# A four-layer graph network on one core: Adj turned a quarter at a time, rows of layer 1 one block nearer to use, bias added in layer 0

## The reference, cut to what matters

```python
# layer 0
gt = adj.T;  deg = gt.sum(1);  d = deg ** -0.5
x = x + (d[:, None] * gt * d[None, :]) @ (h @ W0) + bias
# layer 1
head = (adj > 0) / max(sqrt(row sum of (adj > 0)), 1e-12)
inc = adj + head
x = x + (inc @ h) / inc.sum(-1, keepdims=True)
# layer 2, four heads, the mean of them is added
ht = h @ W;  e = leaky_relu(src[i] + dst[j], 0.01) + adj
x = x + mean over heads of softmax(e) @ ht
# layer 3
x = x + relu(adj @ (binary(h) @ sign(W3).T))
```

## Time and profile before

| | us |
|---|---|
| median of three runs | 764.24 (764.19, 764.24, 768.5) |
| the profiled execution, whole | 766.52 |
| its span | 764.7 |
| mean granted TensorE clock in it | 0.964 |
| TensorE busy | 697.5 |
| VectorE busy | 632.3 |
| ScalarE busy | 480.7 |
| GpSimd busy | 112.5 |

### The profile page before, as it was taken

How to read it: one execution, slowest core, us unless ns; L and a number is a source line. 1 busy time by engine, 2 the same in 40 slices (tenths; PEclk the granted TensorE clock), 3 DMA queues, 4 the chain that set the end, 5 groups by cost and what they waited for, 6 DMA issues and landing times.

```text
span 764.7 us, 16125 instructions
## 1 busy us (share of the span) xinstructions
PE 697.5 (91%) x6480; PEld 587.6 (77%) x6480; DVE 632.3 (83%) x1165; ACT 480.7 (63%) x830; POOL 112.5 (15%) x146
## 2 busy tenths in 40 slices
PE   3988999959999999999990399999999999999998
PEld 3665888848889874488880388887888888888887
DVE  6997687788998737899980499997999999998683
ACT  4996333667887227975540487657686786776751
POOL 4432121311123210011212100211000000000000
PEclk9997999988999999999995699999999999999999
DMA  9886999497879768689999994999411612026591
GB/s 329 304 291 222 426 423 292 173 221 206 183 243 247 163 169 219 173 171 268 254 245 280 313 206 111 206 255 282 167 30 29 193 56 56 4 81 194 203 395 64
DMA packets 146457, 159.54 MB, mean 209 GB/s; under 512 B 90896, under 2 KB 103888, under 8 KB 141904
## 3 DMA queue, kind: packets, MB, share of 16 engines
q1 hardware_dynamic: 127328, 117.10, 51.6%
q0 software_dynamic: 19056, 41.42, 23.6%
HBM read 76.15 MB, written 52.46 MB: 168 GB/s over the span
## 4 chain that ended last, share of the span: by engine, by line
PE 52%; DMA 16%; DVE 15%; ACT 7%; issue 4%; SPq 3%; POOL 2%; ACTq 0%; POOLq 0%; DVEq 0%
DMA adj_t<-arena 8%; PE ps L829 8%; PE ps L831 8%; PE ps L830 8%; PE ps L769 5%; DMA arena<-adj_t 4%; PE ps L871 3%; PE ps L872 3%; DVE arena L1488 3%; DVE arena L1495 3%; DMA arena<-adj_parts 3%; SPq L383 2%; DVE arena L1260 2%; PE ps L717 2%; PE ps L719 2%
## 5 line engine op out<-in xcount | busy, mean ns | idle before, releaser
L829 PE MATMUL ps<-arena 128*128 128x257 f16 x1024 | 280.6, 274 | 32.5 <-DVE arena L1495 32.2
L831 PE MATMUL ps<-arena 128*128 128x257 f16 x1024 | 280.1, 274 | 0.0
L830 PE MATMUL ps<-arena 128*128 128x257 f16 x1024 | 280.0, 273 | 0.0
L1174 ACT ACTIVATE arena<-arena 128x512 f16<-128x512 f32 x252 | 158.2, 628 | 93.5 <-PE ps L831 62.4
L1495 DVE TENSOR_TENSOR arena<-arena 128x512 f16<-128x512 f32 x256 | 175.9, 688 | 40.4 <-ACT arena L1174 40.1
L1488 DVE SCALAR_TENSOR_TENSOR arena<-arena,w_j 128x512 f32<-128x512 f32 x256 | 190.3, 744 | 0.0
L829 PEld LDWEIGHTS ps<-arena 128*128 128x128 f16 x1024 | 100.2, 98 | 47.0 <-ACT arena L1174 33.4
L830 PEld LDWEIGHTS ps<-arena 128*128 128x128 f16 x1024 | 100.5, 98 | 12.7
L831 PEld LDWEIGHTS ps<-arena 128*128 128x128 f16 x1024 | 100.1, 98 | 13.2
L717 PE MATMUL ps<-arena 128*128 128x257 f16 x256 | 71.1, 278 | 3.6 <-DVE arena L1312 3.6
L719 PE MATMUL ps<-arena 128*128 128x257 f16 x256 | 70.5, 275 | 0.0
(11 more groups left out here) (155 smaller groups left out, 1115.6 us busy)
## 6 DMA issues: line engine op xcount, KB each, us to landing
adj_t<-arena POOLq DMA_DIRECT2D x32, 1024.0 KB, 8.3
arena<-in_adj_dram SPq DMA_DIRECT2D x32, 512.0 KB, 6.0
arena<-in_adj_dram SPq DMA_DIRECT2D x16, 1024.0 KB, 5.2
adj_parts<-arena SPq DMA_DIRECT2D x16, 1024.0 KB, 25.8
arena<-adj_t SPq DMA_DIRECT2D x64, 256.0 KB, 6.1
arena<-adj_t SPq DMA_DIRECT2D x16, 1024.0 KB, 7.1
x<-arena POOLq DMA_DIRECT2D x15, 512.0 KB, 6.2
arena<-u_rows SPq DMA_DIRECT2D x4, 1024.0 KB, 14.2
```

Of the source, the lines that this page charges most:

```text
L829: mm(ps[:, bank, 0:DE], hi, ht_hi[:, head, j, 0:DE], start=s, stop=False)
L830: mm(ps[:, bank, 0:DE], hi, ht_lo[:, head, j, 0:DE], start=False, stop=False)
L831: ins = mm(ps[:, bank, 0:DE], lo, ht_hi[:, head, j, 0:DE], start=False, stop=e)
L1174: nc.scalar.activation(p_hi[:, j % 4, :], prob[:, j % 4, :], copy).then_inc(p_hi_done, 1)
```

## The change

Four things are edited.

1. SP turns groups 4 to 7, loads e of quarter 1, turns 8 to 11, loads quarter 2, turns 12 to 15, loads quarter 3, and issues the two early loads of layer 3 last. WIDEN_AFTER spreads the widenings over heads 0 to 9 instead of 0 to 5; its waits on the pieces of quarter 3 ahead of the early loads go, as `load_e(3)` has them.
2. In layer 1 sign, count, fill, transposes and parts of a row come one iteration later than before (t + 5, t + 5, t + 4, t + 3, t + 3), and row 5 isn't counted in layer 0 any more. The five buffers stay.
3. TensorE multiplies groups 0 to 2 of rows 0 and 1, then group 3 of row 0, then group 3 of row 1.
4. The bias tile lies over `hrelu` instead of in g_hi's area. It is loaded after Adj, ahead of the writes of `nat`, once h @ W0 has read `hrelu`. GpSimd adds it after the powers of the degrees and before the loop with `inverse_root1`; VectorE waits for each tile's add in layer 0, and ScalarE no longer waits for it.

```diff
-        b0_bc = view(G0 + 7 * KB, [D], F32)
         hrelu = view(160 * KB, [2, D], F32)
+        b0_bc = view(160 * KB, [D], F32)
...
-        COUNTS = (1, 2, 9, 10, 11, 14)
+        COUNTS = (1, 2, 9, 10, 11)
...
-        WIDEN_AFTER = {0: (6, 7), 1: (8, 9), 2: (10, 11), 4: (12, 13), 5: (14, 15)}
+        DMA_ROWS = ()
+        PE_ROWS = [t for t in range(AHEAD, NB) if t not in DMA_ROWS]
+        WIDEN_AFTER = {0: (6,), 1: (7,), 3: (8,), 4: (9, 10), 5: (11,), 7: (12,), 8: (13, 14), 9: (15,)}
...
-            sp.dma_start(b0_bc, b0_d.partition_broadcast(P)).then_inc(bias_in, 16)
...
             for t in range(2):
                 load_rows(t)
+            sp.wait_ge(h0_lo_done, NB)
+            sp.dma_start(b0_bc, b0_d.partition_broadcast(P)).then_inc(bias_in, 16)
...
-            for n in range(QB, 3 * QB):
-                turn_adj(n)
             for q in range(1, NQ):
-                if q == 2:
-                    for n in range(3 * QB, 4 * QB):
-                        turn_adj(n)
-                if q == NQ - 1:
-                    for g in range(TG):
-                        sp.wait_ge(wide[g], 16 * NQ)
-                    for i in range(2):
-                        sp.dma_start(adjt_early[i], adjt_dram[i]).then_inc(adjt_in[4 + i], 16)
+                for g in range(TG):
+                    turn_adj(QB * q + g)
                 load_e(q)
+            for i in range(2):
+                sp.dma_start(adjt_early[i], adjt_dram[i]).then_inc(adjt_in[4 + i], 16)
...
-            pool.wait_ge(bias_in, 16)
-            for t in range(NB):
-                pool.wait_ge(relu0, t + 1)
-                nc.gpsimd.tensor_tensor(x[:, t, :], x[:, t, :], b0_bc, ALU.add).then_inc(bias_added, 1)
             pool.wait_ge(deg_copied, 1)
             for lo, hi in DINV_PIECES:
                 nc.gpsimd.tensor_tensor(dinv_in[:, lo:hi], deg[:, lo:hi], neg_half[:, lo:hi], ALU.pow
                                         ).then_inc(dinv_done, 1)
+            pool.wait_ge(bias_in, 16)
+            for t in range(NB):
+                nc.gpsimd.tensor_tensor(x[:, t, :], x[:, t, :], b0_bc, ALU.add).then_inc(bias_added, 1)
...
-                if t + 6 < NB:
-                    inverse_count(t + 6)
+                if t + 5 < NB:
+                    inverse_count(t + 5)
...
-            for t in range(NB):
+            for groups in (range(NB // TG - 1), (NB // TG - 1,)):
+                for t in range(2):
+                    for g in groups:
+                        products1(t, g)
+            for t in range(2, NB):
                 for g in range(NB // TG):
-                    if AHEAD <= t + 4 < NB:
-                        transpose_group(t + 4, g)
+                    if t + 3 in PE_ROWS:
+                        transpose_group(t + 3, g)
                     products1(t, g)
...
-            act.wait_ge(bias_added, NB)
...
             for t in range(NB):
-                more = AHEAD <= t + 4 < NB
+                more = t + 3 in PE_ROWS
                 if more:
-                    part_high(t + 4, 0)
-                if t + 6 < NB:
-                    sign(t + 6)
+                    part_high(t + 3, 0)
+                if t + 5 < NB:
+                    sign(t + 5)
...
-            dve.wait_ge(bias_added, NB)
-
             def layer0(t):
                 b = t % 2
+                dve.wait_ge(bias_added, t + 1)
                 dve.wait_ge(y_ps, t + 1)
...
-                if t + 5 < NB:
-                    fill(t + 5)
+                if AHEAD <= t + 4 < NB:
+                    fill(t + 4)
```

More of the change, by code:

```diff
@@ L687, in transpose_group @@
             def transpose_group(t, g):
-                n = 4 * (t - AHEAD) + g
+                n = 4 * PE_ROWS.index(t) + g
                 if g == 0:
@@ L703, in products1 @@
                 bank = ACC[t % 3]
-                if t >= AHEAD:
-                    pe.wait_ge(part_lo_done, 4 * (t - AHEAD) + g + 1)
+                if t in PE_ROWS:
+                    pe.wait_ge(part_lo_done, 4 * PE_ROWS.index(t) + g + 1)
                 elif g == 0:
-                    pe.wait_ge(inc_in[t], 32)
+                    pe.wait_ge(inc_in[t % AHEAD], 32 * (t // AHEAD + 1) if t < AHEAD else 64)
                 if g == 0 and t >= 3:
@@ L774, in _ @@
             pe.wait_ge(w2_lo_done, 4)
-            pe.wait_ge(part_lo_done, 4 * (NB - AHEAD))
+            pe.wait_ge(part_lo_done, 4 * len(PE_ROWS))
             pe.wait_ge(l1_taken, NB - 1)
@@ L1024, in _ @@
             for t in range(NB):
-                more = AHEAD <= t + 4 < NB
+                more = t + 3 in PE_ROWS
                 if more:
-                    part_high(t + 4, 0)
-                if t + 6 < NB:
-                    sign(t + 6)
+                    part_high(t + 3, 0)
+                if t + 5 < NB:
+                    sign(t + 5)
                 if more:
-                    part_high(t + 4, 1)
+                    part_high(t + 3, 1)
                 if t >= 2:
@@ L1034, in _ @@
                 if more:
-                    part_high(t + 4, 2)
+                    part_high(t + 3, 2)
                 if t >= 1:
@@ L1038, in _ @@
                 if more:
-                    part_high(t + 4, 3)
-                if t + 6 < NB:
-                    count(t + 6)
+                    part_high(t + 3, 3)
+                if t + 5 < NB:
+                    count(t + 5)
                 if t == 0:
@@ L1358, in fill @@
                     dve.wait_ge(nat_sent[1], 32)
-                if t >= AHEAD + 2:
-                    dve.wait_ge(t_ps, 4 * (t - AHEAD - 2) + 4)
+                if t - 2 in PE_ROWS:
+                    dve.wait_ge(t_ps, 4 * PE_ROWS.index(t - 2) + 4)
                 v.scalar_tensor_tensor(inc[:, t % 2, :], mask[:, t % 2, :], c_row[:, t:t + 1], rows[t % 3],
@@ L1426, in _ @@
                 if more:
-                    part_low(t + 4, 0)
+                    part_low(t + 3, 0)
                 if t >= 1:
@@ L1430, in _ @@
                 if more:
-                    part_low(t + 4, 1)
+                    part_low(t + 3, 1)
                 if t == 0:
                     inc_low(4)
-                if t + 5 < NB:
-                    fill(t + 5)
+                if AHEAD <= t + 4 < NB:
+                    fill(t + 4)
                 if more:
-                    part_low(t + 4, 2)
-                    part_low(t + 4, 3)
+                    part_low(t + 3, 2)
+                    part_low(t + 3, 3)
                 if t >= 1:
```

## The result

The changed kernel took 730.93 us in the median of four runs (728.57 to 732.13), the kernel before 766.37 beside it (764.19 to 768.52): a ratio of 0.9534 [0.9489, 0.9579]. The forecast was 728, with a range of 721 to 741.

The account below looks back on a forecast made before the run. TensorE, busy 91% of 764.7 us, was taken to lose time where it stands still, mainly a 32.8 us ScalarE wait for adj_t. -32.4 - 3.4 - 0.5 = -36.3 us gave 728 us on the median, range 721 to 741.

Parts of the forecast that it names:

- Part 1: Layer 2, Adj turned a quarter at a time: stalls of 31.9 and 2.0 us go, 1.5 us is added; -32.4 us.
- The clean price of four heads: Layer 2: 86.12 us between ScalarE scales four heads apart, from the last pair, which has no stall at its boundary.
- The rebuilt queue: Layer 2: transposes, widenings and loads re-timed from measured landings, such as 6.3 us per transpose; lows 11 us early.
- the margin stays: Layer 2: low parts land 11 us before load_e(2) piece 3 wants them, and likewise one boundary later, shifted 84.6 us.
- the second rival: Layer 2: pieces of e land late at each boundary, 3 x 2.5 us more, 735.5 us; chance 0.12.
- Part 2: Layer 1, rows one block nearer and first two blocks together: -5.2 + 1.8 = -3.4 us.
- part 3: Bias loaded and added later: VectorE's work on Adj less stretched and 0.13 MB less loaded first; -0.5 us.
- catches up there, by 130 or 135: Layer 0: VectorE, delayed by the late bias, makes it up before rows 2 to 4 of layer 1 are finished.
- Layer 1 giving nothing (the first): Layer 1: the 6.7 us wait for fill(5) grows and TensorE restarts slow; 731.5 us, 736 with slow bias; chance 0.13.
- The series of widenings that doesn't fit (the third): Layer 2: at 25 us a group, boundaries 1/2 and 2/3 lose 16 us each, 760 us; chance 0.03, plus 0.03 for 740-757.
- The fourth: Layer 2: load_e(1) piece 3 waits for group 7, behind group 1's head on POOL; 7 us lost, 735 us; chance 0.02.
- the bad landing at each: Layer 2: by the skill's rule taken strictly, each boundary costs 3.0 us, making the sum 7.5 us higher.

Follow-up runs that it names:

- e1: The kernel before with only SP's new order in layer 2 and the new WIDEN_AFTER: 733.08 us, ratio 0.9552.
- f2: The changed kernel without the bias edits: 732.02 us, ratio 0.9526.
- e6: The changed kernel with GpSimd's bias adds taken apart, four ahead of the inverse roots and the others one by one behind them: 732.46 us, ratio 0.9532.
- e7: The changed kernel with row 5 counted in layer 0 again and its fill put ahead of the last inc_low: 731.76 us, ratio 0.9517.
- e10: The changed kernel with the bias loaded at the start into its own tile, adds still behind the powers of the degrees: 732.87 us, ratio 0.9542.
- f4: The changed kernel with bias adds taken apart, row 5 counted in layer 0 and its fill put first: 728.69 us, ratio 0.9484.
- f1: The changed kernel without layer 1's row shift and joint start of rows 0 and 1: 732.54 us, ratio 0.9531.
- e3: The kernel before with only layer 1's row shift and the joint start of rows 0 and 1: 766.95 us, ratio 1.0005.
- e8: The changed kernel with WIDEN_AFTER packed in pairs after heads 3, 4, 7 and 8: 738.83 us, ratio 0.9653.
- e2: The kernel before with only the bias edits (loaded late, added behind the powers of the degrees): 765.98 us, ratio 1.001.
- e5: The kernel before with layer 1's rows one iteration later, but row 0 done alone as before: 768.25 us in one run.

## Why the prediction was right

**Part 1, forecast -32.4 us, measured -30.8.** The step that carried it holds as worked out: the queue's order put `load_e(1)` 35 us late, and with the load free boundary 0/1 costs nothing. The clean price of four heads, 86.12 us, was if anything too high by 0.2 (85.9 for the first difference in eight profiles with the spread order). e1 shows it alone. The rebuilt queue was good to some 4 us: piece 0 of quarter 1 was put at 389.5 on a mark of 391.96 and came at 385.84 on a mark of 388.24, 2.4 ahead in both. The lows of groups 8 to 11 were put at 442, 456, 466 and 479. They were issued at 429.56, 443.95, 456.01 and 470.92, and with the median landing of 8.6 us this is 438, 453, 465 and 480. The head marks themselves came 2.5 to 3.7 us sooner than in the rebuild, so against them the last low part was some 3 us late.

**The mis-sized term: "the margin stays".** I had 0.5 us for each boundary, 1.5 in all; against the clean 86.12 they cost -0.2, 1.1 and 2.2, that is 3.1. The last one is where a step failed in this execution. GpSimd's timeline after, ahead of boundary 2/3, and then ScalarE's exp of piece 3:

```profile
543.69 1.28 POOL L543 DMA_DIRECT2D adj_t<-arena  x1 [4.44 <-DMA adj_t<-arena]
544.45 1.43 POOL L580 DMA_DIRECT2D x<-arena  x1
559.28 0.77 POOL L539 DMA_DIRECT2D adj_t<-arena  x1 [13.39 <-DMA arena<-adj_parts]
565.80 1.28 POOL L543 DMA_DIRECT2D adj_t<-arena  x1 [5.75 <-DMA adj_t<-arena]
```

```profile
581.06 0.72 ACT L1049 ACTIVATE arena<-arena,amax 128x512 f32<-128x512 f32 x1 [4.38 <-DMA arena<-adj_t]
```

The transposes of L384 between 530 and 560 us:

```profile
DMA to landing us min/median/max: 5.8/7.4/15.9
```

Group 15's last transpose, issued at 543.1, took 15.9 us to land beside group 14's accumulate and a head's add. Its low part went out at 565.8, where the shifted rebuild has 479 - 8.9 + 84.6 = 554.7. The margin of 11 us was used up and ScalarE waited 4.38 us. I had used 6.3 us, the median of a transpose, and a median is no bound for a chain with 11 us to spare. The kind of cost was that of the second rival, at one boundary of three and 2.2 us of its 2.5.

It was not always so. Two things have to be told apart. The rebuild has this low part going out 6.5 us ahead of head 10's mark (554.7 and 561.2). In e1, f2, e6, e7, e10 and f4 it goes out 2.8 to 4.1 us ahead of it: so some 3 us of the margin of 11 were lost there too, and the last difference is 86.1 to 87.1 us. The other loss is the long landing. It came in the changed kernel and in f1, where a transpose took 21.3 us, the low part went out 5.7 us behind the mark and the last difference is 90.64. All eight have group 14's accumulate and a head's add at this place, and in the six the slowest transpose between 525 and 565 us took 7.9 to 9.5 us. So lying beside them is not enough for a long landing, and its cause stays open. In all, the three boundaries cost between -0.5 us (f4) and 7.7 us (f1), below 1 us in six of the eight kernels; the forecast of 1.5 lies within that, and 3.1 is one execution's.

**Part 2, forecast -3.4, measured -0.85 in the changed kernel, -2.3 to -2.7 where the bias stays early (e3, f2).** Start of layer 1, TensorE's timeline:

```profile
164.07 0.28 PE L713 MATMUL ps<-arena 128*128 128x257 f16 x1 [1.55 <-DVE arena L1311]
...
172.54 0.69 PE L693 MATMUL ps<-ident,arena 128*128 128x128 f32 x2 [6.64 <-DVE arena L1359]
```

and VectorE's fill of row 5:

```profile
170.13 2.35 DVE L1359 SCALAR_TENSOR_TENSOR arena<-arena,c_row 128x2048 f32<-128x2048 f16 x1 [0.78 <-POOL c_row L527]
```

An idle time of 6.7 us was forecast, 6.64 came; c_row is on the path as said; the lower clock as said. But layer 0 ended at 153.3, not at 156.5, and the transposes came only 1.3 us before the forecast 173.85. The step that failed stands in part 3: "catches up there, by 130 or 135; rows 2 to 4 of layer 1 are finished later than that". VectorE did catch up at 132.7. Behind that, however, tiles 12 to 15 are a chain of ScalarE, GpSimd and VectorE in series, in which TensorE's three us of lead were lost: the last h1_lo comes 1.55 us late, and row 5 is 19.2 us behind layer 0's end, not 17.5 as in e3, f2, e6 and e10. e6 shows a part of it: adds apart, 17.5 again, layer 1 at 123.05. The other thing that the rebuild lacked is GpSimd's wait in `add_low(1)`. The rebuild let iterations 2 to 4 keep their lead and then TensorE set the pace; in every trace layer 1 ends at a nearly fixed distance behind that issue. Where the bias stays early, the issue comes 4.9 to 5.4 us sooner with part 2 (forecast: a lead of 5.2) and 2.6 to 2.7 us are given back behind it (forecast: 1.8). In the changed kernel it comes 3.3 us sooner than before and 2.5 are given back. The term is one of a few us with a scatter as large: e8, with the same layer 1, has +2.3 against before.

**Part 3, forecast -0.5, measured -2.9 ahead of layer 1.** The adds of the changed kernel, and VectorE's split of Adj:

```profile
L509 POOL TENSOR_TENSOR x<-x,arena x16: 718/724/1708, 75.2 to 87.5; 128x256 f32<-128x256 f32 x16
...
L1259 DVE SCALAR_TENSOR_TENSOR arena<-arena x32: 1212/1219/1226, 12.5 to 65.1; 128x1024 f16<-128x1024 f32 x32
```

The adds took 0.72 us in the median, not 0.99, and the bias had landed 2 us before the forecast; the first inverse root came at 88.2, between the forecast 93 and no delay. TensorE never stood for a tile. What was too small is the first term: the degrees came 1.9 us sooner. I had priced VectorE's shorter operations (its longest split is 1.23 us now, 1.75 before) and 0.13 MB less; e10 has the first of these without the gain, so it would be the second, the place of the bias load, that I seem to have priced too low by its bytes; the profiles nearly touch, as said. Layer 0's 1.0 us isn't explained: it took 86.6 to 87.3 us in the profiles with the early load and 85.9 to 86.9 in those with the late one.

The two misses have opposite signs, -2.9 for -0.5 and -0.85 for -3.4, and they cancel: 3.7 us ahead of the projection, 3.9 forecast. That the sum was near there is luck; with e8's layer 1 it would have missed by over 3 us. What was known is the 32 us.

**The rivals.** Layer 1 giving nothing (the first) came nearer than its chance of 0.13 says: 0.85 of 3.4 us. Its reason, that the wait for fill 5 grows with count 5 on its path, is a true description of the place, but the wait did not grow (6.64 us), and in e7 taking it away did not shorten layer 1. The series of widenings that doesn't fit (the third) did not come: four groups fitted ahead of boundary 1/2, where the boundary cost 1.1 us, and in two profiles of eight they were late by a few us at 2/3. The fourth did not come. The boundaries cost 3.1 us in all, at two of three, where the bad landing at each would have been 9.0. The rule of the Trainium skill that I weighed there ("DMA: Bandwidth & Descriptors", "Queues, rings and completion order": each DMA engine takes turns between the queue rows, a packet at a time) agrees in direction with the 15.9 us landing beside an accumulate. The 7.9 to 9.5 us of six kernels at the same place show that this alone is not enough for it, and taken strictly at each boundary the rule overstates the cost. The adds ended at 88.2, one of 1.71 us among others of 0.72. The Trainium skill's rule that a VectorE instruction with two SBUF inputs and a GpSimd one that reads SBUF exclude each other ("SBUF — State Buffer", "Who interferes with whom") would have ended them near 105, by the estimate made from the earlier trace rows. It hardly came to bear: the adds began at 75.24 us, as VectorE ended its last g_lo (75.3), and beside them VectorE ran two of the maxima (L1316). Where they met the rule's direction shows: these two took 1.75 and 1.74 us, the next ones 1.22, and one add took 1.71. Likewise in the Adj phase VectorE's splits lost their long ones when the adds left.

## What to carry to other kernels

Read an in-order queue for what stands ahead of the transfer that is late: moving eight transposes of work that nobody needed yet was worth 33 us, at no work saved. When two in-order queues feed each other, spread the slow items on both; packing them moves the wait to the next user of the same queue (8 us in e8). A gain ahead of a stall that DMAs time cannot be measured until the stall is gone; and a hole in TensorE that is closed (e7) gives nothing back where a later wait for a landing, here with an inverse root queued behind it, sets when the stage ends. When two kernels are compared by the stages of one profile each, look first for two profiles in which that stage is the same code: layer 1 differed by 3.2 us between two such.

## What the runs showed of the hardware that was not expected

A DMA transpose whose landing is 5.9 us in the median took 15.9 in the changed kernel and 21.3 in f1, beside an accumulate and a head's add that elsewhere left it at 9.5 or less; and an accumulate of 1 MB between 7.2 and 14.5 (median 8.6). One and the same GpSimd add of 128x256 float32 took 0.72 us in the median while VectorE ran two of its maxima in 13 us (1.75 and 1.74 us each, the next ones 1.22), against up to 1.77 in the Adj phase of before; VectorE's split of Adj has no value over 1.23 us once the adds are gone. A chain of 16 transposes and the widenings between them lasted 93.9 to 96.5 us in four kernels in which it was not changed (before, e2, e3, e5).
